# One-hots of a whole expert group in one 16-bit operation, and one transposition moved, in a 64-expert layer

## The reference

```
scores = jax.nn.softmax(xf @ gate_w.T, axis=-1)
topk_w, topk_idx = jax.lax.top_k(scores, K)                      # K = 6 of E = 64
...
pos = jnp.arange(T * K, dtype=jnp.int32) - offsets[sorted_e]     # slot of the token in its expert
buf_tok = jnp.full((E, CAP), T, jnp.int32).at[sorted_e, pos].set(sorted_tok, mode='drop')
gx = xp[buf_tok]                                                 # gather, CAP = 64 rows for each expert
gu = jnp.einsum('ech,ehi->eci', gx, gate_up_proj)
g, u = jnp.split(gu, 2, axis=-1)
hid = jax.nn.silu(g) * u
eo = jnp.einsum('eci,eih->ech', hid, down_proj) * buf_w[..., None]
routed = jnp.zeros((T + 1, h), x.dtype).at[buf_tok.reshape(-1)].add(eo.reshape(-1, h))[:T]
shared = jax.nn.silu(xf @ shared_gate_w.T) * (xf @ shared_up_w.T) @ shared_down_w.T
return (routed + shared).reshape(b, s, h)
```

## Time and profile before

| | |
|---|---|
| Median of 3 runs | 2062.59 us (2057.7 to 2067.89) |
| The profiled execution | 2056.34 us, its span 2054.6 us |
| Mean granted TensorE clock | 0.919 of full speed |
| Busy: PE, DVE, ACT, POOL | 85%, 62%, 41%, 26% of the span |
| Block a, from the first expert products to the read-back of results | about 818 to 933 us of the span |
| Block b, the same | about 1688 to 1803 us |

### The profile page before, as it was taken

The page is one execution under the profiler, slowest core; times in us unless marked ns, Lnnn a source line. Parts: engine busy times, 40 slices in busy tenths (PEclk is TensorE's granted clock), DMA queues, the critical chain, the costliest instruction groups (busy, mean ns, idle before and its releaser), DMA issues. The chain is left out here.

```text
span 2054.6 us, 39921 instructions
## 1 busy us (share of the span) xinstructions
PE 1737.0 (85%) x15101; PEld 1162.3 (57%) x15101; DVE 1266.8 (62%) x3523; ACT 838.5 (41%) x1859; POOL 539.7 (26%) x670
## 2 busy tenths in 40 slices
PE   3786779997799996776799999999998997869579
PEld 1345654464456564454466676676666774636456
DVE  6868651435464334854688989889888338552741
ACT  4523321311573211332576767767766103410120
POOL 1012410232585322471321221222221005700300
PEclk7897999998899998897799999999999898999779
DMA  7100000321600422774100101101010427740000
...
DMA packets 55283, 156.59 MB, mean 76 GB/s; under 512 B 12899, under 2 KB 29881, under 8 KB 50822
## 3 DMA queue, kind: packets, MB, share of 16 engines
...
...
## 5 line engine op out<-in xcount | busy, mean ns | idle before, releaser
L2745 DVE SCALAR_TENSOR_TENSOR l_heads_taps<-l_heads_padded,l2a_conv,l_heads_taps 128x1024 f32<-128x1024 f32 x144 | 183.9, 1287 | 7.8 <-ACT l_heads_taps L2601 5.5
L2385 PE MATMUL l_heads_ps_p<-xnT,l2a_w 128*128 128x512 f32 x256 | 128.9, 618 | 2.9 <-PEq L66 2.9
L2385 PE MATMUL l_heads_bank<-xnT,l2a_w 128*128 128x512 f32 x256 | 127.3, 611 | 0.0
L205 PE MATMUL norm_turn<-zeros,ident 128*128 128x512 f32 x120 | 61.6, 665 | 47.3 <-PEq L66 44.0
L1910 POOL TENSOR_SCALAR l_heads_e<-l_heads_e,l_heads_inverse 128x128 f32<-128x128 f32 (+1 forms) x128 | 94.9, 761 | 24.7 <-DVE l_heads_inverse L2040 24.7
...
L2944 POOL TENSOR_TENSOR l_heads_e<-l2a_table,l_heads_row 128x512 f32<-128x512 f32 x32 | 33.3, 1042 | 185.7 <-DVE l_heads_first L2756 183.9
L2955 POOL TENSOR_SCALAR l_heads_rstd<-l_heads_mean_var 128x8 f32<-128x8 f32 x16 | 3.9, 243 | 281.5 <-DVE l_heads_mean_var L2824 281.5
L205 PEld LDWEIGHTS norm_turn<-zeros,ident 128*128 128x128 f32 x120 | 24.5, 213 | 78.6 <-issue 78.6
L1995 ACT ACTIVATE l_heads_e<-l_heads_logit,l_heads_shift 128x128 f32<-128x128 f32 (+1 forms) x128 | 56.6, 443 | 24.8 <-DVE l_heads_shift L2026 24.8
L438 PE MATMUL l_ffn_a_ps_gate<-xnT,l_w 128*115 128x512 f32 x44 | 28.8, 790 | 39.7 <-DVE l_w L569 38.2
L2385 PEld LDWEIGHTS l_heads_ps_p<-xnT,l2a_w 128*128 128x128 f32 x256 | 43.7, 194 | 31.8 <-issue 29.9
...
## 6 DMA issues: line engine op xcount, KB each, us to landing
...
```

Source lines behind the costliest of these rows:

```text
L205: pe.matmul(turn[:, i % KC, (i // KC) % HALVES, :], core.ident[:], core.zeros[:, 0:HALF], start=True, stop=True)
L2385: mm = pe.matmul(out, w[b][:, which, c, :], core.xnT[:, c, half * HALF:(half + 1) * HALF], start=(c == 0), stop=(c == KC - 1))
L2745: dve.scalar_tensor_tensor(out=taps[which][:], in0=padded[which][:, :, j:j + SEQ], scalar=conv[p % 2][:, which, j:j + 1], in1=taps[which][ ...
```

## The change

Four edits, all in `l2_experts_stage`, so each acts in both blocks:

1. `hot` is laid out with the expert innermost: [tile, slot, expert] in place of [pair, tile, expert of the pair, slot]. `slot` is widened from 64 to 64 x 8 elements, so that both inputs and the output have a step of one element in the innermost index. Before, `slot_of` was read with a step of 0 there.
2. A group's one-hots are one operation of 4096 elements for groups 1 to 7 in place of eight of 512 (or four of 1024). Group 0 keeps one for each pair, now 512 pairs of two elements.
3. The products read `hot` with a step of 8 elements (16 bytes) from one slot to the next. Those of group 0 are split into two for each tile, with 64 weight columns each.
4. PE does `turn_x(0)` ahead of `index(2)`, and DVE does the one-hots of group 3 behind `hidden(0)` and no longer ahead of it.

```diff
-        slot = st.sb("slot", [P, S], BF16)
+        slot = st.sb("slot", [P, S, EG], BF16)
-        hot = [st.sb(f"hot{b}", [P, PAIRS, TILES, 2, S], BF16) for b in range(2)]
+        hot = [st.sb(f"hot{b}", [P, TILES, S, EG], BF16) for b in range(2)]
...
+        def hot_of(g, q, i):
+
+            return hot[g % 2][:, i, :, 2 * q:2 * q + 2].rearrange("p s j -> p j s")
...
-            pool.tensor_copy(slot[:], number[:]).then_inc(const_ready, 1)
+            pool.tensor_copy(slot[:], number[:].unsqueeze(2).broadcast_to([P, S, EG])).then_inc(const_ready, 1)
...
                     for i in range(TILES):
-                        mm = pe.matmul((bank_l, bank_r)[q % 2][:, 6 * q:6 * q + 6], hot[0][:, q, i].rearrange("p j s -> p (j s)"),
-                                       parts[:, i, 2 * q:2 * q + 2, :].rearrange("p j i -> p (j i)"), start=(i == 0), stop=(i == TILES - 1))
+                        for j in range(2):
+                            mm = pe.matmul((bank_l, bank_r)[q % 2][BOTH[j], 6 * q:6 * q + 6], hot[0][:, i, :, 2 * q + j],
+                                           parts[:, i, 2 * q:2 * q + 2, :].rearrange("p j i -> p (j i)"),
+                                           start=(i == 0), stop=(i == TILES - 1))
...
                         mm = pe.matmul(bank_l[ROWS * q:ROWS * q + 6, 0:P], parts[:, i, e:e + 2, :].rearrange("p j i -> p (j i)"),
-                                       hot[g % 2][:, q, i].rearrange("p j s -> p (j s)"),
+                                       hot_of(g, q, i),
...
             pe.wait_ge(shared_taken, 2 * UNITS)
+            turn_x(0)
             index(2)
             turn_i(2)
-            turn_x(0)
...
-            def one_hot(g, q):
+            def one_hot(g, pairs=slice(0, PAIRS)):
                 if g >= 2:
-                    dve.wait_ge(i_filled, q + 1 if g == 2 else count_of(g - 2))
...
+                    dve.wait_ge(i_filled, PAIRS if g == 2 else count_of(g - 2))
+                some = slice(2 * pairs.start, 2 * pairs.stop)
+                width = some.stop - some.start
+                dve.tensor_tensor(hot[g % 2][:, :, :, some],
+                                  slot[:, :, some].unsqueeze(1).broadcast_to([P, TILES, S, width]),
+                                  slot_of[:, :, g * EG + some.start:g * EG + some.stop].unsqueeze(2)
+                                  .broadcast_to([P, TILES, S, width]),
+                                  ALU.is_equal).then_inc(hot_ready, 1)
...
+            one_hot(1)
             locate(0, slice(3, 4))
...
             locate(1)
-            for q in range(PAIRS):
-                one_hot(2, q)
+            one_hot(2)
             locate(2)
-            for q in range(PAIRS):
-                one_hot(3, q)
             for g in range(GROUPS):
...
+                if g == 0:
+                    one_hot(3)
                 if g + 3 < GROUPS:
                     locate(g + 3)
                 if g + 4 < GROUPS:
-                    for q in range(PAIRS):
-                        one_hot(g + 4, q)
+                    one_hot(g + 4)
```

More of the change, by code:

```diff
@@ L3124, in count_of @@
             return PAIRS + g
-        def hot_count(g, q):
-            return PAIRS * g + q + 1 if g < 2 else 2 * (PAIRS * (g - 1) + q + 1)
+        def hot_of(g, q, i):
+            return hot[g % 2][:, i, :, 2 * q:2 * q + 2].rearrange("p s j -> p j s")
         @block.sync
@@ L3407, in settled @@
                 dve.wait_ge(step_done, steps[0])
-            def one_hot(g, q):
+            def one_hot(g, pairs=slice(0, PAIRS)):
                 if g >= 2:
-                    dve.wait_ge(i_filled, q + 1 if g == 2 else count_of(g - 2))
-                e = g * EG + 2 * q
-                pieces = 1 if g < 2 else 2
-                for i in range(0, TILES, TILES // pieces):
-                    some = slice(i, i + TILES // pieces)
-                    dve.tensor_tensor(hot[g % 2][:, q, some],
-                                      slot[:].unsqueeze(1).unsqueeze(1).broadcast_to([P, TILES // pieces, 2, S]),
-                                      slot_of[:, some, e:e + 2].unsqueeze(3).broadcast_to([P, TILES // pieces, 2, S]),
-                                      ALU.is_equal).then_inc(hot_ready, 1)
+                    dve.wait_ge(i_filled, PAIRS if g == 2 else count_of(g - 2))
[6 more added lines that the diff above has]
+                                  ALU.is_equal).then_inc(hot_ready, 1)
             def locate(g, pairs=slice(0, PAIRS)):
@@ L3480, in _ @@
             settled()
-            one_hot(0, 0)
-            one_hot(0, 1)
+            one_hot(0, slice(0, 1))
+            one_hot(0, slice(1, 2))
             locate(0, slice(0, 1))
-            one_hot(0, 2)
+            one_hot(0, slice(2, 3))
             locate(0, slice(1, 2))
-            one_hot(0, 3)
+            one_hot(0, slice(3, 4))
             locate(0, slice(2, 3))
-            one_hot(1, 0)
+            one_hot(1)
             locate(0, slice(3, 4))
@@ L3495, in add_shared @@
                                          op0=ALU.mult, op1=ALU.add).then_inc(shared_added, 1)
-            for q in range(1, PAIRS):
-                one_hot(1, q)
             locate(1)
-            for q in range(PAIRS):
-                one_hot(2, q)
+            one_hot(2)
             locate(2)
-            for q in range(PAIRS):
-                one_hot(3, q)
             for g in range(GROUPS):
```

4 lines of the change are left out of this document (2 added, 2 removed).

## The result

The changed kernel takes 2072.09 us (median of 7 runs, 2069.04 to 2076.05) against 2062.59 us (7 runs) before. The ratio is 1.0045, 95% interval 1.0029 to 1.0062: 6 to 13 us slower, where 7 were forecast. The profiled execution took 2072.09 us, its span 2070.2 us, the mean granted clock is 0.921.

The account below looks back on a forecast made before the run. GpSimd's train of gathers and scatters was taken as the bound. A start 0.9 us later and 2.7 of new holds made 3.6 a block, 7 for both: 2070 us against the 2062.6 median, range 2055 to 2085.

Parts of the forecast that it names:

- The bound: GpSimd's closed train of 20 gathers and 32 scatters sets each block's end, 71.2 us from 860.85.
- The first rival: VectorE was the bound: five groups each 2.8 us shorter, 28 for both blocks, 2035 us; 8%.
- The new one-hot: VectorE's 4096-element operation takes 2.25 us in place of 5.05, between bounds of 2.2 and 4.36.
- The last rival: The one-hot still runs at one element a time, 4.36 us: 28 us for both blocks, 2091 us; 8%.
- The holds: GpSimd transfers begun inside a one-hot wait until 0.86 us behind its end: 6.4 us a block, 2.7 new.
- The rival by which the operation does not hold GpSimd: Longer one-hots hold GpSimd not at all or briefly: 5.6 us gained for both blocks, 2057 us; 14%.
- The strided products: Index products reading hot at 16-byte steps cost 0.3 us for each of two on the path, 0.6.
- the slow rival: Strided reads make products slow, deciding once 32 take over 3 us: 21 us for both blocks, 2084 us; 14%.
- I count nothing: Group 0's doubled short products, 0.4 to 4.4 us for four pairs, priced at nothing as hidden by a data wait.
- The earlier transposes pay for the later one-hots and no more: Ahead of the train: up(0) 2.85 us earlier, group 3's one-hots behind hidden(0), take_at(3) only 0.3 later.
- The sum: take_at of group 3 0.9 us later plus 2.7 of new holds: 3.6 us a block, 7 for both.
- The train: GpSimd's gathers and scatters from group 3 on, starting near 862, closed up at 0.30 us; gaps would refute it.

Follow-up runs that it names:

- E1: The changed kernel with edit 4 undone (group 0's transposes behind index(2), group 3's one-hots ahead of hidden(0)): 2071.5 us, 1.0050 to the kernel before.
- E2: The kernel before with only the two moves of edit 4, on its old one-hots: 2069.49 us, 1.0043 to the kernel before.
- E3: The changed kernel with the one-hots of groups 1 to 7 in four operations of 1024 elements each: 2068.17 us, 1.0036 to the kernel before.
- E5: The changed kernel with pair-innermost one-hots (four operations a group, products reading at 4-byte steps) and the old order: 2055.03 us, 0.9967 to the kernel before.
- E8: E5 with a group's one-hots in one operation of 4096 elements, places first copied by pair: 2062.28 us, 1.0001 to the kernel before.
- E7: The kernel before with only turn_x(0) moved ahead of index(2): 2058.42 us, 0.9989 to the kernel before.
- E4: The changed kernel with pair-innermost one-hots (four operations a group, products reading at 4-byte steps), new order kept: 2063.5 us, 1.0012 to the kernel before.

## Why the prediction was right, and where its steps were wrong

**The bound** was read rightly. The four kernels whose trains ended later in both blocks together by 4 us or more (changed, E1, E2, E3) were slower, and E5, whose trains ended 8.8 earlier, was faster; the others lie too near to 1 to be told apart. No variant gained by VectorE's saved 2.8 us a group alone: E8, with that saving, the old order and no slow reads, is at 1.0001. The first rival (2035) is refuted.

**The new one-hot** was taken as 2.25 us and took 2.28. The last rival falls.

**The holds.** This mechanism was right and was isolated by E8 against E5, 7 us for both blocks. The first hold was put at 1.6: the gather at 862.15 took 2.50 in place of 0.95, 1.55. The four together were put at 6.1 (with the pick 6.4) and measured 2.50 + 1.95 + 2.51 + 2.55 less their unheld 0.95 to 1.00, 5.7. New against the trace before is less than the 2.7 forecast in block a: the stretch column rose by 1.7 there, and by 2.5 in block b. The rival by which the operation does not hold GpSimd is refuted. The Trainium skill's remark on which it stood ("SBUF — State Buffer", section "Who interferes with whom": tensor_tensor was not seen to stall such a DMA) does not fit this trace: here an indirect transfer's issue stalled under tensor_tensor by up to 2.1 us.

**The strided products** are the term that was mis-sized. It was put at 0.3 us for each 32 and at nothing for group 0. Measured: 2.04 in place of 1.02 at the low clock and of 0.62 at the high one, so 1.0 to 1.4 each. It lay between the forecast's value and the slow rival's condition of 3 us. For group 0 a pair's 16 products took 1.12 in place of 0.35, so 3.1 for the four, inside the bounds of 0.4 to 4.4. "I count nothing" is the step that failed: the cover that was to hide them was not there, since they lie ahead of the gather and not beside its wait. The last gather of group 0 was issued at 838.52, 13.1 behind `slot_of`, where it was 9.9. Its `take_at` came at 837.75, 12.4 behind `slot_of`, where it was 9.2, because TensorE, which has no gap there, now gets through a pair in 2.94 us in place of 1.98. The hold of 3.01 on the gather ahead moved it by 0.4 at most. It landed 8.2 later, at 846.75, 21.4 behind `slot_of` in place of the 18.9 assumed. How long such a landing takes differs between executions (for this gather, in block a, 6.1 us in E3 and 10.7 in E2), so the place of the landing is no fixed price. Alone (E8 to E1) the step costs 10 us of both blocks, of which up to 1 us a block can be that of group 0's one-hots. With what the Trainium skill says ("SBUF — State Buffer", section "Door 1: The DMA port swizzle", a penalty for each new 16-byte line) the products agree in direction: 0.63 us with four slots in such a line, 2.0 with one, 0.62 with eight.

**The order.** "The earlier transposes pay for the later one-hots and no more" was right for the changed kernel by the medians (E1 to changed: 1.0050 to 1.0045, the intervals overlap). Its profiled blocks say +4 for both, so a cost of a few us stays open. Its first half was exact: E7 moves up(0) by 2.9. But the account is no property of the move. Where the one-hots and products around it are fast, the transposes have nothing to gain and the open one-hots cost in full: from E5 to E4 index(3) starts 3.0 and 4.0 later, and the ratio goes from 0.9967 to 1.0012, 9 us.

**The sum.** take_at(3) was due 32.4 behind `slot_of` and came at 35.8. Of the 3.4, 1.8 stood at the end of `hidden(0)`, 29.7 against 27.8 (27.5, and the 0.3 taken for index(2)): the landing was 2.4 late, index(2) with its 2.04 made up(0) 0.8 later than the 0.3 allowed, and up(0) itself, which the clock happened to favour (2.83 against 4.28 before), gave 1.4 back. The other 1.6 are the products of index(3) and the turn behind it. In block b take_at(3) came 2.0 later than forecast.

The train was forecast 2.7 longer. In block b it is 2.8 longer, 2.5 of that by stretched transfers. In block a it is 3.5 longer, 1.7 by stretch and 1.8 by the two gaps of 1.34 and 1.09. These were not foreseen: the forecast had said that the train would close up at 0.30, and that gaps would make it wrong. What stands ahead of them is the stretch behind the late transposes. In the view by windows the columns are: window and length in us, busy time of PE, PEld, DVE, ACT and POOL, granted clock of TensorE, share of the DMA engines, GB/s. First the changed kernel:

```profile
911.00:921.00 10.00, 9.92 (x58) 6.86 (x58) 0.35 (x1) 2.69 (x6) 7.56 (x9) 0.56 0.34 113
```

and then of the kernel before:

```profile
912.00:922.00 10.00, 8.56 (x86) 6.08 (x80) 2.41 (x6) 4.43 (x10) 7.56 (x9) 1.00 0.30 107
```

After TensorE had waited 3.42 us for rows, it was granted 0.56 of full speed, near the lower of its two levels (1.2 of 2.4 GHz), where before it did not wait ahead of this group and had 1.00. down and up took 3.68 and 4.42 against 1.95 and 2.77, 3.4 more. By this reading, wait and clock together ate the margin that TensorE had over the train. It is argued and not shown. The kernel before has such a wait too, one group earlier, with a down of 3.68 and an up of 3.03 behind it, and no gap follows:

```profile
898.68 1.94 PE L3256 MATMUL l_ffn_a_bank_x<-ident,l_ffn_a_xg 128*128 128x128 f32 x8 [4.66 <-DMA l_ffn_a_xg<-l_xn_rows,l_ffn_a_take_at]
```

In block b of the changed kernel a wait of 1.94 (at 1787.52) with products of 3.68 and 3.13 behind it leaves no gap either, and E1, with the same layout, has none. So the gaps stand in one block of one execution, and their cause stays open.

In all, 3.6 us a block were forecast, and by the profile it is 7.8 and 5.7, by the medians 4.7. The forecast of +7 lies within the measured +6 to +13. That it is right as a total is in part luck: the train's start was 3.4 and 2.0 later than forecast, and block a, at 7.8, lies outside the forecast's own 1.2 to 7 for a block. What these terms lacked is within the spread of executions.
